# Local attention on one core: root of the norms, order of scores and values, score tiles and buffers changed together

## What is computed

```
qkv = x @ Wqkv                      # 16 heads of 64
q = l2norm(q) * qs;  k = l2norm(k) * ksc
q = q * cos * scale + rotate_half(q) * sin * scale
k = k * cos / scale + rotate_half(k) * sin / scale
sim  = einsum('bhwie,bhwje->bhwij', bq, bk2) * 8.0
sim  = where(mask, -max, sim)       # 32 keys back and the own ones
attn = softmax(sim);  out = attn @ bv2;  return out @ Wo
```

## Time and profile before

| | |
|---|---|
| median of three runs | 5192.08 us |
| profiled execution: time | 5195.5 us |
| profiled execution: span of its instructions | 5193.7 us |
| TensorE matmul / VectorE / ScalarE / GpSimd busy, share of the span | 76 / 73 / 50 / 42% |
| mean granted TensorE clock | 0.806 |
| start of the first instruction of local layer 1, of local layer 6 | 223.1, 2131.2 us |

### The profile page before, as it was taken

One profiled execution on the slowest core, in us unless ns is written; L12 is line 12 of the kernel. 1 busy time (PEld: TensorE's weight loads), 2 busy tenths in 40 slices (PEclk: granted clock), 3 DMA queues, 4 the chain that ended last, 5 costly groups with the idle time before them and its releaser, 6 DMA issues. The chain is left out here.

```text
span 5193.7 us, 75861 instructions
## 1 busy us (share of the span) xinstructions
PE 3971.8 (76%) x25476; PEld 2536.7 (49%) x25476; DVE 3768.7 (73%) x7356; ACT 2570.9 (50%) x6832; POOL 2171.7 (42%) x1600
## 2 busy tenths in 40 slices
PE   5389799799799799799777767956666666588897
PEld 2166466466466466466343343433333333355564
DVE  5799599599599598698354544399999999832343
ACT  2188488488488488488222121233333333326343
POOL 0177277277276376376120310066666666500000
PEclk8699899899899899899777687855555555567898
DMA  0011111111111111111000000000000000000000
GB/s 17 28 41 42 38 42 42 37 42 42 37 41 41 39 40 42 37 42 43 28 1 9 1 25 1 0 1 1 1 1 1 1 1 1 1 7 1 22 1 9
DMA packets 48634, 109.67 MB, mean 21 GB/s; under 512 B 8944, under 2 KB 9200, under 8 KB 46704
## 3 DMA queue, kind: packets, MB, share of 16 engines
q1 hardware_dynamic: 48240, 104.66, 6.6%
HBM read 31.23 MB, written 1.05 MB: 6 GB/s over the span
## 5 line engine op out<-in xcount | busy, mean ns | idle before, releaser
L1085 POOL TENSOR_TENSOR slabs<-slabs 128x512 f32<-128x512 f32 x768 | 975.4, 1300 | 368.7 <-DVE slabs L949 368.7
L1782 DVE MAX8 slabs<-slabs 128x8 f32<-128x512 f32 x1084 | 691.6, 679 | 57.4 <-ACT slabs L1719 57.4
L1808 POOL TENSOR_SCALAR slabs<-slabs 128x512 f32<-128x512 f32 x256 | 400.3, 1564 | 470.4 <-DVE slabs L1788 470.4
L1074 POOL TENSOR_TENSOR slabs<-slabs 128x768 f32<-128x768 f32 x192 | 341.9, 1781 | 567.9 <-DVE slabs L926 567.9
L623 PE MATMUL psum<-slabs 128*128 128x512 f32 x768 | 413.2, 665 | 214.7 <-DVE slabs L949 149.5
L1703 ACT ACTIVATE slabs<-slabs 128x512 f32<-128x512 f32 x316 | 211.6, 719 | 727.8 <-DVE slabs L1788 727.8
L854 ACT ACTIVATE slabs<-slabs 128x96 f32<-128x96 f32 x1536 | 551.4, 360 | 37.2 <-PE psum L667 35.7
L1641 PE MATMUL psum<-constants,slabs 128*128 128x128 f32 x1264 | 305.5, 407 | 299.7 <-POOL slabs L1811 299.3
L1784 DVE MATCH_REPLACE8 slabs<-slabs 128x512 f32<-128x512 f32 x768 | 513.0, 675 | 0.0
L1632 PE MATMUL psum<-slabs 8*128 8x512 f32 (+1 forms) x632 | 346.5, 1087 | 164.2 <-ACT slabs L1719 164.1
L659 PEld LDWEIGHTS psum<-weights,slabs 128*128 128x128 f32 x3072 | 372.2, 192 | 101.3 <-issue 86.1
(11 more groups left out here) (392 smaller groups left out, 8378.0 us busy)
## 6 DMA issues: line engine op xcount, KB each, us to landing
slabs<-slabs SPq DMA_DIRECT2D x192, 192.0 KB, 2.5
slabs<-slabs SPq DMA_DIRECT2D x192, 128.0 KB, 2.5
slabs<-F1A SPq DMA_DIRECT2D x7, 2176.0 KB, 8.4
slabs<-slabs SPq DMA_DIRECT2D x144, 64.0 KB, 2.1
slabs<-F1F SPq DMA_DIRECT2D x6, 580.5 KB, 4.2
slabs<-S SPq DMA_DIRECT2D x4, 645.0 KB, 6.5
weights<-M SPq DMA_DIRECT2D x1, 2184.0 KB, 9.4
weights<-R SPq DMA_DIRECT2D x2, 1079.5 KB, 5.5
```

What stands on the lines that cost most here:

```text
L1074: nc.gpsimd.tensor_tensor(probs, probs, scale, ALU.mult).then_inc(probs_ready, 1)
L1085: nc.gpsimd.tensor_tensor(out[:, at, :], normed[:, at, :], table, ALU.mult).then_inc(rope_done, 1)
L1782: nc.vector.max(eight, work[side] if k else scores[slot + side]).then_inc(picked[b], 1)
L1808: nc.gpsimd.tensor_scalar(kept[n % 2], scores[slot], tops[:, slot, TOPK - 1:TOPK], None, ALU.is_ge).then_inc(kept_ready, 1)
```

## The change

All of it is in the local attention.

- The lower bound of the sum of squares goes from VectorE (L938) to ScalarE, which now does `Relu`, `Ln`, `Exp` and `Square` of 16 columns. VectorE's three steps become two: `measure` and `refine`; the factor -0.5 and the lift go into the rotary tables.
- The factor 8 goes into the query tables, and the maxima come out negated, so that L978 goes.
- Scores are taken with 16 products on quarter-array tiles (64 rows, 64 output partitions), without the zero half of `qBD`; queries are copied in one instruction; heads and windows lie in another order, and the mask of the first tile is one instruction.
- `normed` has two buffers.
- The order of the calls in the loops of TensorE, ScalarE and VectorE changes; queries are turned one round later, values are copied one round later.

```diff
-    qBD = m.slab(7)[:, 256:1280].rearrange("p (n w h q) -> p n w h q", n=PAIRS, w=2, h=2)
+    qT = m.slab(7)[:, 256:768].rearrange("p (n q) -> p n q", n=PAIRS)
...
-            nc.gpsimd.memset(m.slab(7)[:, 256:1280], 0.0)
...
-    normed = m.slab(12)[:, 1024:2048].rearrange("p (h d) -> p h d", d=HD1)
+    normed = [a.rearrange("p (h d) -> p h d", d=HD1) for a in (m.slab(12)[:, 1024:2048], m.slab(7)[:, 768:1792])]
...
             def score(u):
...
                 for n in range(GROUPED):
-                    c, k = n // 2, n % 2
-                    keys = kT[:, PAIRS * half + c, t * P + k * WINDOW:t * P + k * WINDOW + KEYS]
-                    last = nc.tensor.matmul(SCORES[:, n // 4, n % 4, :], qBD[:, c, k, :, :], keys, start=True, stop=True)
+                    c, h = n // 2, n % 2
+                    for k in range(2):
+                        keys = kT[64 * h:64 * h + 64, PAIRS * half + c, t * P + k * WINDOW:t * P + k * WINDOW + KEYS]
+                        queries = qT[64 * h:64 * h + 64, c, k * WINDOW:k * WINDOW + WINDOW]
+                        last = nc.tensor.matmul(ps[k * WINDOW:k * WINDOW + WINDOW, 4 + h, KEYS * c:KEYS * c + KEYS], queries, keys,
+                                                start=True, stop=True)
...
             for i in range(UNITS + 6):
                 if i < UNITS:
                     project(i)
+                if 0 <= i - 2 < UNITS:
+                    turn_queries(i - 2)
                 if 0 <= i - 5 < UNITS:
                     weigh(i - 5)
...
                 if 0 <= i - 4 < UNITS:
                     turn_probs(i - 4, 1)
+                if 0 <= i - 2 < UNITS:
+                    score(i - 2)
                 if 0 <= i - 3 < UNITS:
                     values(i - 3)
-                if 0 <= i - 2 < UNITS:
-                    score(i - 2)
-                if 0 <= i - 1 < UNITS:
-                    turn_queries(i - 1)
...
             def root_of_sum(u):
-                act.wait_ge(root_step, ROOT_STEPS * u + 2)
-                nc.scalar.activation(logs, sums, ACT.Ln, scale=LIFT).then_inc(logged, 1)
-                act.wait_ge(logged, u + 1)
-                nc.scalar.activation(root, logs, ACT.Exp, scale=-0.5).then_inc(rooted, 1)
+                act.wait_ge(root_step, ROOT_STEPS * u + 1)
+                nc.scalar.activation(logs, sums, ACT.Relu, scale=LIFT, bias=m.tiny[:, 2:3]).then_inc(logged, 1)
+                act.wait_ge(logged, 3 * u + 1)
+                nc.scalar.activation(logs, logs, ACT.Ln, bias=m.tiny[:, 3:4]).then_inc(logged, 1)
+                act.wait_ge(logged, 3 * u + 2)
+                nc.scalar.activation(root, logs, ACT.Exp, scale=-0.5).then_inc(logged, 1)
+                act.wait_ge(logged, 3 * u + 3)
+                nc.scalar.activation(logs, root, ACT.Square).then_inc(rooted, 1)
...
             for i in range(UNITS + 5):
                 if i < UNITS:
                     square(i)
-                if 0 <= i - 5 < UNITS:
-                    copy_context(i - 5)
+                if 0 <= i - 2 < UNITS:
+                    copy_queries(i - 2)
+                if 0 <= i - 4 < UNITS:
+                    copy_values(i - 4)
+                if i < UNITS:
+                    root_of_sum(i)
                 if 0 <= i - 4 < UNITS:
                     copy_probs(i - 4, 0)
                 if 0 <= i - 2 < UNITS:
                     copy_keys(i - 2)
-                if i < UNITS:
-                    root_of_sum(i)
+                if 0 <= i - 5 < UNITS:
+                    copy_context(i - 5)
                 if 0 <= i - 3 < UNITS:
                     exponential(i - 3)
                 if 0 <= i - 4 < UNITS:
                     copy_probs(i - 4, 1)
-                if 0 <= i - 3 < UNITS:
-                    copy_values(i - 3)
-                if 0 <= i - 1 < UNITS:
-                    copy_queries(i - 1)
...
-                nc.vector.tensor_scalar(sums, sums, 1e-24, None, ALU.max).then_inc(root_step, 1)
+            def measure(u):
+                dve.wait_ge(rooted, u + 1)
+                nc.vector.scalar_tensor_tensor(out=grown, in0=sums, scalar=LEAST, in1=logs, op0=ALU.max, op1=ALU.mult).then_inc(root_step, 1)
+            def refine(u):
+                dve.wait_ge(root_step, ROOT_STEPS * u + 2)
+                nc.vector.scalar_tensor_tensor(out=root, in0=grown, scalar=-3.0 / LIFT, in1=root, op0=ALU.add, op1=ALU.mult).then_inc(root_step, 1)
             def normalise(u):
...
-                if u >= 1:
-                    dve.wait_ge(rope_done, 4 * u)
+                if u >= 2:
+                    dve.wait_ge(rope_done, 4 * (u - 1))
...
+            def find_maxima(u):
                 dve.wait_ge(masked_step, MAX_STEPS * u + 1)
-                nc.vector.tensor_reduce(tops, masked, axis=AX.X, op=ALU.max).then_inc(masked_step, 1)
-                dve.wait_ge(masked_step, MAX_STEPS * u + 2)
-                nc.vector.tensor_scalar(shifts, tops, -8.0, None, ALU.mult).then_inc(shift_ready, 1)
+                nc.vector.tensor_reduce(shifts, masked, axis=AX.X, op=ALU.max, negate=True).then_inc(masked_step, 1)
...
             for i in range(UNITS + 6):
+                if 0 <= i - 2 < UNITS:
+                    rope(i - 2, 0, q_roped)
                 if 0 <= i - 4 < UNITS:
                     total(i - 4)
-                if 0 <= i - 2 < UNITS:
-                    rope(i - 2, 1, k_roped)
                 if 0 <= i - 3 < UNITS:
                     mask_scores(i - 3)
                 if i < UNITS:
                     sum_squares(i)
+                    measure(i)
+                if 0 <= i - 3 < UNITS:
+                    find_maxima(i - 3)
                 if 0 <= i - 6 < UNITS and i % 2 == 1:
                     residual(i - 6)
+                if i < UNITS:
+                    refine(i)
+                    normalise(i)
                 if 0 <= i - 1 < UNITS:
-                    rope(i - 1, 0, q_roped)
-                if i < UNITS:
-                    normalise(i)
+                    rope(i - 1, 1, k_roped)
```

More of the change, by code:

```diff
@@ L477 @@
 UNITS = 2 * (TOK // P)
+LIFT, LEAST = 2.0 ** 20, 1e-24
+QK_SCALE = 8.0
 GROUPED = 2 * PAIRS
@@ L550, in local_layer @@
     logs, grown, root = (small[:, 16 + 16 * i:32 + 16 * i] for i in range(3))
-    tops, denom, inverse, shifts = (small[:, 80 + 8 * i:88 + 8 * i] for i in range(4))
+    denom, inverse, shifts = (small[:, 80 + 8 * i:88 + 8 * i] for i in range(3))
     v = [m.slab(16 + n // 2)[0:KEYS, 1024 * (n % 2):1024 * (n % 2) + 1024].rearrange("p (k d) -> p k d", k=2) for n in range(4)]
@@ L679, in weigh @@
                         last = nc.tensor.matmul(ps[rows, 3, WINDOW * n:WINDOW * n + WINDOW], v[u % 4][:, k, c * P + 64 * h:c * P + 64 * h + 64],
-                                                turned[0:KEYS, c, k, rows], start=True, stop=True)
+                                                turned[0:KEYS, PAIRS * h + c, k * WINDOW:k * WINDOW + WINDOW], start=True, stop=True)
                 last.then_inc(pv_product, 1)
@@ L831, in copy_queries @@
                     act.wait_ge(score_product, u)
-                for h in range(2):
-                    rows = slice(64 * h, 64 * h + 64)
-                    nc.scalar.activation(qBD[rows, :, :, h, :], QT[rows, :, :, :], ACT.Copy).then_inc(qT_copied, 1)
+                nc.scalar.activation(qT, QT, ACT.Copy).then_inc(qT_copied, 1)
             def copy_values(u):
@@ L846, in copy_probs @@
                     act.wait_ge(pv_product, u)
-                nc.scalar.activation(turned[0:KEYS, 2 * part:2 * part + 2, :, :], PT, ACT.Copy).then_inc(pT_copied, 1)
+                nc.scalar.activation(turned[0:KEYS, 4 * part:4 * part + 4, :], PT, ACT.Copy).then_inc(pT_copied, 1)
             def exponential(u):
-                act.wait_ge(shift_ready, u + 1)
+                act.wait_ge(masked_step, MAX_STEPS * u + 2)
                 if u >= 1:
@@ L853, in exponential @@
                 for n in range(GROUPED):
-                    last = nc.scalar.activation(probs[:, n, :], masked[:, n, :], ACT.Exp, bias=shifts[:, n:n + 1], scale=8.0,
+                    last = nc.scalar.activation(probs[:, n, :], masked[:, n, :], ACT.Exp, bias=shifts[:, n:n + 1],
                                                 accum_out=denom[:, n:n + 1])
@@ L1084, in rope @@
                         table = tables[:, t, 2 * side + k:2 * side + k + 1, :].broadcast_to([P, 8, HD1])
-                        nc.gpsimd.tensor_tensor(out[:, at, :], normed[:, at, :], table, ALU.mult).then_inc(rope_done, 1)
+                        nc.gpsimd.tensor_tensor(out[:, at, :], normed[u % 2][:, at, :], table, ALU.mult).then_inc(rope_done, 1)
             for i in range(UNITS + 3):
@@ L2475, in rotary_tables @@
     cos, sin = np.cos(freqs), np.sin(freqs) * sign
-    kinds = np.stack([a.astype(f) for a in (cos * scale, sin * scale, cos * inv, sin * inv)], 1)
-    return f(1024) * kinds.reshape(4, P, 4, HD1).transpose(1, 0, 2, 3).reshape(P, -1)
```

(5 more changed lines are left out.)

46 lines of the change are left out of this document (17 added, 29 removed).

## The result

The kernel after takes 5058.18 us (median of 4 runs, 5050.46 to 5061.08), the kernel before on the same chip 5193.4; the ratio is 0.9734, with a 95% interval of 0.9717 to 0.9751. The forecast was 5117 us in a range of 5040 to 5180. The profiled execution of after took 5050.46 us (span 5048.7), 145.0 less than that of before.

What follows compares the result with a forecast made beforehand. TensorE was taken to bound rounds with `project_out`, VectorE the others. The new loop (8.81 us) and TensorE's 8.99 average 8.90, with holds 8.94 against 9.42, over 26 rounds and 6 layers 75 us: 5117 us, range 5040 to 5180.

Steps and rivals of the forecast that it cites:

- What bounds before: Steady rounds of the local layers: TensorE bounds those with `project_out` (9.36 us), VectorE those without (9.42 us).
- X: TensorE's time for `score` as 32 quarter-tile records: 1.55 us, taken between 1.15 and 1.74, instead of 1.92.
- The new loop: Projection, square, root, `copy_probs`, second half of `turn_probs`, `score`, `values`, next projection: 7.26 + X = 8.81 us.
- VectorE's relief: VectorE loses L938, L978 and one small root step, 2.0 us a unit: 8.99 us fall to about 7.0.
- The holds: VectorE's small steps wait for the GpSimd instruction in flight; 0.04 us added to the mean round, giving 8.94.
- rival 2: `measure` and `refine` on VectorE are often held by GpSimd: mean round 9.15 to 9.45, 5150 to 5195 us; 18%.
- GpSimd's loop: GpSimd and VectorE: key and query halves roped, total, `finish_probs`, four multiplications; about 8.3 us, the next late bound.
- The head of a layer: First five rounds of a layer, with the attention part's end: no change, within 2 us a layer either way.
- 1: `score` on TensorE: tiles overlap better, X near 1.15, mean round about 8.55, gain 136 us, 5056 us; 20%.
- 3: `score` on TensorE: quarter tiles run one after the other, X = 3.84, rounds 11.1 and 11.3, 5470 us; 8%.
- 4: TensorE empties before and after `score` at the tile-shape change: 0.3 to 0.5 us more, 5165 to 5195 us; 8%.
- Signs: Trace signs of a right forecast: squares 8.8 to 9.0 apart, score 1.4 to 1.7, VectorE idle over 1.5 us.

Runs made afterwards that it cites:

- tiles_alone: The kernel after with the old call order and old root, keeping quarter tiles, single query copy, negated maxima, one mask instruction, two buffers: 5289.26 us, ratio 1.0187.
- score_twice: The kernel after with all of `score` issued twice, 64 records for 32, same results: 5176.49 us, ratio 0.9971.
- no_refinement: The kernel after without VectorE's two small steps `measure` and `refine`, their factor taken out of the rotary tables: 5041.07 us, ratio 0.9713.
- probs_early: The kernel after with `copy_probs(i - 4, 0)` moved ahead of `root_of_sum(i)` on ScalarE: 5202.71 us, ratio 1.0023.

## Why the prediction was right in direction and short in size

- *What bounds before* (TensorE with `project_out`, VectorE without): not contradicted. tiles_alone adds what the argument lacked: a shorter TensorE, with VectorE's holds left, is slower, with a longer wait and a lower clock.
- *X, the score's group*: the term that was mis-sized. Forecast 1.55 us between 1.15 and 1.74, measured 0.89, below the lower bound: 28 ns a record of 96 columns (and 0.66 us for the next 32, 21 ns each, in score_twice), less than the 36 ns of `weigh`'s 64 columns on half-width tiles. The bound assumed that four quarter tiles overlap no better than two halves.
- *The new loop*: right, as score_twice and no_refinement together show. With X = 0.89 and 0.18 more for the root (Relu to Ln and Ln to Exp take 0.34 us each from start to start, not the 0.25 of Ln to Exp in the earlier trace rows) it is 7.26 + 0.18 + 0.89 = 8.33; TensorE with `project_out` is 9.36 - 1.92 + 0.89 = 8.33. The squares stand 8.35 apart. The wait of `turn_probs`' second half for the copy is there, with 1.59 us. That the first sum hits so closely is in part luck: step by step `turn_probs` to `score` took 0.57 us and not 0.37, since `score` waits for the copy of the keys, which the path leaves out, and X to the start of `values` 0.82 and projection to square 1.92 instead of 0.89 and 2.02 took most of it back.
- *VectorE's relief*: forecast 9.0 to 7.0 us, measured 6.23 in these rounds. What the count left out: the rope additions, which take 688 ns in the mean of L964 now that GpSimd has nothing in flight there. ScalarE: 7.9 forecast, 7.88 measured; but it was counted as busy time only. With the 0.30 us that it waits for the sum of the squares its queue nearly fills the round of 8.33, and the forecast has no loop for it.
- *The holds* (0.04 us in the mean): right, but by a narrow margin. `measure`, forecast ready at 3.32 us after the square, is ready 3.46 after it (689.53 to 692.99) and slips in, because GpSimd is late as well: its second multiplication ends 3.7 us after the square and not 3.4. The two errors cancel, which is luck; 0.2 us late costs 1.03 us a round (probs_early). The forecast priced a miss at 1.2 us in rival 2 and took as relief that a longer round moves the phase away. In probs_early the phase did not move: each round misses again, 9.38 us apart.
- *GpSimd's loop, about 8.3 us*: not reached. `finish_probs` took 1.47 us and not 1.81, and `total`, ahead of it on VectorE, waits 0.32 us for the last exponential's sum (697.35), so this loop would close in some 8.0.
- *The head of a layer* (within 2 us with the tail): 3.1 us slower, 3.5 with the tail, outside the margin. The five rounds took 45.5 us in no_refinement too (580.25 to 625.75), so it is not the small steps; the rows show the lower clock in its third and fourth round, and it was not tried further.
- *Rivals*: 1 came true, with X lower still and its VectorE hold absent. Its 5056 us match by luck: the steady rounds gained 168 us and not 136, and head and tail gave 21 back. 2 is what the neighbouring orders do. 3 is refuted by the 0.89 us. 4: no gap before or behind `score`; `values` starts 0.82 us behind the group's start. The rule cited there (the Trainium skill, "TensorEngine Tiling (Array Packing)", Key Properties), that a change of tiling mode drains the engine, shows no cost here. By the rule cited in rival 2 (the Trainium skill, "GPSIMD Engine Reference", Key points) the `scalar_tensor_tensor` steps are held as well: the trace agrees, with 1.06 and 1.19 us instead of 0.25.
- *Signs*: of those named for a right forecast, the squares (8.8 to 9.0 us apart) and the score's group (1.4 to 1.7) came out lower, and the projection starts behind `values` and `normalise` together; VectorE's idle time (2.1 us a round) and the wait of `turn_probs` are as named.

The sum: forecast 8.94, less 0.66 of X, less 0.04 of holds, plus 0.09 for the root (it lies in every second round's bound) is 8.33; 26 x 6 x (9.42 - 8.346) = 168 us, less 6 x 3.5 at head and tail = 147 (145 measured in the profiled execution).

## What to carry to other kernels

Before an engine is relieved, look at who will wait: in the old order the shorter `score` became a wait of some 2 us every second round, mostly with a halved clock behind it. Where small VectorE instructions on SBUF operands share a round with long GpSimd ones, lay both out on a time axis from the same start and compare each request with GpSimd's ends: the price is a step, 0 or nearly the length of a whole instruction, and moving a 0.6 us copy ahead of the root cost 145 us of 5058. Leave one part of a change out at a time before calling any part the gain: here each of three parts, taken out alone, left a kernel slower than before.

## What the runs showed of the hardware that was not expected

- 32 single-precision records of 64 rows, 64 columns of weights and 96 moving columns, on the four quarters of the array in turn, take 0.89 us, 28 ns each, and 64 take 1.55 (score_twice). The same scores as 16 full-array records took 1.92 us.
- `scalar_tensor_tensor` of 16 columns is held to the end of GpSimd's multiplication in flight, 1.19 us for 0.25; with multiplications of half the length its longest duration in the rows above is 0.77 us.
- After waits of 2.0 to 2.2 us without a matmul the clock mostly fell to the 1.2 GHz level within 2 us (eight of ten in tiles_alone; 0.53 over the projection at 722.99), after the waits of 1.59 us in every second round of after it stayed at 1.00.
- A GpSimd multiplication of 512 columns takes 1.24 us, of 256 columns 0.69: the part that doesn't shrink is 2 x 0.69 - 1.24 = 0.14 us (worked out from the two).
